# Softplus as one activation, softmax exponentials joined to decay bursts, and down products of 25 experts turned: a macaron layer on one core

## The reference

```
x = x + 0.5 * moe(layernorm(x))
x = x + mamba(layernorm(x))
x = x + 0.5 * moe(layernorm(x))          # the same weights again

moe(x):                                   # 8 experts, all of them for every token, F = 512
  router = softmax(x @ w_router);  gates = softmax(x @ w_gating / 0.1)
  h[e] = silu(x @ w_gate[e]) * (x @ w_up[e])
  cw = router * gates;  cw = cw / (sum(cw) + 1e-9)
  out = sum over e of (h[e] @ w_down[e]) * cw[:, e]

mamba(x):                                 # 256 inner channels, 16 states, conv of 4 taps
  xs, z = split(x @ W_in);  xc = silu(conv(xs) + conv_b)
  dbl = xc @ W_x;  dt = softplus(dbl[:64] @ W_dt + b_dt);  B, C = the rest of dbl
  dA = exp(dt * A), A = -exp(A_log);  dBx = dt * xc * B
  h_t = dA_t * h_(t-1) + dBx_t;  y_t = sum over states of h_t * C_t
  out = ((y + xc * D) * silu(z)) @ W_out
```

## Time and profile before

| | |
|---|---|
| median of 3 runs | 1244.83 us (1244.51 to 1245.08) |
| profiled execution, first to last instruction (span) | 1243.0 us |
| median less this span (launch and end around it) | 1.8 us |
| PE busy | 1237.4 us, 7212 products |
| DVE busy | 1143.1 us |
| ACT busy | 1004.7 us |
| POOL busy | 450.6 us |

### The profile page before, as it was taken

The page is one execution under the profiler, slowest core; times in us unless marked ns, Lnnn a source line. Parts: engine busy times, 40 slices in busy tenths (PEclk is TensorE's granted clock), DMA queues, the critical chain, the costliest instruction groups (busy, mean ns, idle before and its releaser), DMA issues.

```text
span 1243.0 us, 20366 instructions
## 1 busy us (share of the span) xinstructions
PE 1237.4 (100%) x7212; PEld 1066.6 (86%) x7212; DVE 1143.1 (92%) x1353; ACT 1004.7 (81%) x2022; POOL 450.6 (36%) x574
## 2 busy tenths in 40 slices
PE   9999999999999999999999999999999999999999
PEld 7888888888888888888888888888888888888887
DVE  5958799999998999999999999998999999998877
ACT  7678888988887989887988989898888987865554
POOL 0021144335462443543534425344453344531000
PEclk9999999999999999999999999999999999999999
DMA  8312488798877879878889787977778779881222
GB/s 232 97 30 44 86 176 176 154 184 171 168 159 155 173 150 196 168 165 165 171 175 184 162 179 149 190 163 154 153 165 175 163 155 194 169 179 35 61 52 59
DMA packets 118135, 184.59 MB, mean 148 GB/s; under 512 B 11280, under 2 KB 34448, under 8 KB 118032
## 3 DMA queue, kind: packets, MB, share of 16 engines
q0 software_dynamic: 54384, 99.11, 45.7%
q1 hardware_dynamic: 63648, 84.16, 25.3%
HBM read 81.46 MB, written 2.69 MB: 68 GB/s over the span
## 4 chain that ended last, share of the span: by engine, by line
PE 90%; ACT 3%; DVE 3%; DMA 2%; issue 2%; POOL 0%; DVEq 0%; ACTq 0%; POOLq 0%
PE PS L1070 27%; PE PS L961 18%; PE PS L964 18%; PE PS L962 18%; PE PS L1066 2%; PE PS L1062 1%; PE PS L1064 1%; PE PS L1128 1%; DMA XT<-YE 1%; DVE HB L1310 1%; PE PS L1113 1%; DMA Y<-HS 1%; PE PS L997 1%; DVE HS L1408 1%; ACT HB L1521 1%
## 5 line engine op out<-in xcount | busy, mean ns | idle before, releaser
L1070 PEld LDWEIGHTS PS<-WD,HB 128*128 128x128 f32 x3424 | 422.3, 191 | 23.7 <-issue 1.5
L1070 PE MATMUL PS<-WD,HB 128*128 128x128 f32 x3424 | 424.5, 275 | 0.0
L1310 DVE TENSOR_TENSOR HB<-PS,HB 128x1024 f32<-128x1024 f32 (+1 forms) x336 | 322.6, 961 | 77.2 <-PE PS L964 56.1
L1521 ACT ACTIVATE HB<-PS 128x512 f32<-128x512 f32 x512 | 293.6, 596 | 101.7 <-PE PS L964 99.6
L1712 POOL DMA_DIRECT2D Y<-HS x252 | 220.8, 957 | 343.8 <-DVE HS L1416 164.0
L961 PE MATMUL PS<-XH,WG 128*128 128x512 f32 x509 | 221.3, 435 | 0.0
L961 PE MATMUL PS<-XH,WU 128*128 128x512 f32 x512 | 205.3, 401 | 0.7 <-DVE HB L1310 0.5
L964 PE MATMUL PS<-XH,WU 128*128 128x512 f32 x512 | 201.2, 393 | 0.0
L964 PE MATMUL PS<-XH,WG 128*128 128x512 f32 x509 | 200.8, 395 | 0.0
L962 PE MATMUL PS<-XH,WU 128*128 128x512 f32 x512 | 200.5, 392 | 0.0
L962 PE MATMUL PS<-XH,WG 128*128 128x512 f32 x509 | 199.2, 391 | 0.0
(11 more groups left out here) (168 smaller groups left out, 1466.1 us busy)
## 6 DMA issues: line engine op xcount, KB each, us to landing
BCB<-BCD SPq DMA_DIRECT2D x128, 512.0 KB, 5.2
Y<-HS POOLq DMA_DIRECT2D x252, 256.0 KB, 6.0
XT<-YE POOLq DMA_DIRECT2D x106, 256.0 KB, 5.0
YE<-CWD SPq DMA_DIRECT2D x20, 256.0 KB, 4.5
AT<-YE POOLq DMA_DIRECT2D x14, 256.0 KB, 3.3
WD<-in_L_ffn_w_down_dram SPq DMA_DIRECT2D x8, 256.0 KB, 6.2
XT<-in_L_attn_x_dram SPq DMA_DIRECT2D x7, 256.0 KB, 6.5
out_dram<-XT SPq DMA_DIRECT2D x7, 256.0 KB, 5.7
```

Of the source, the lines that this page charges most:

```text
L1070: z = pe.matmul(part(g, j), HB[:, i % NH, j * P:(j + 1) * P], WD[:, e, c, :], start=c == 0 and j == 0, stop=c == FC - 1 and j == SUB - 1)
L1310: v.tensor_tensor(H, PS[:, NG + i % 2:NG + i % 2 + n, :], H, ALU.mult).then_inc(S["v_h"], 1)
L1521: a.activation(HB[:, i % NH, :], gate(i), ACT.Silu).then_inc(S["a_sil"], 1)
```

## The change

Three things are changed.

- Softplus is one activation. b_dt writes v + bias to DX (Identity), b_soft makes Softplus of it into XS. The sum on DVE, the accumulating DMA of tiles 1 to 3 and the list ADDED go. Decays wait for b_soft.
- The exponentials of a position's softmaxes are asked for, and the next burst of decays issues them ahead of its own, if one comes before the planner's PE clock has moved on by PATIENCE = 25; otherwise, and while no tile's decays are open, they are issued alone as before.
- TURNS has experts 1 to 7 in positions 1 and 14, 25 in all where there were 20.

```diff
-ADDED = (1, 2, 3)
-SUMMED = 10.0
+PATIENCE = 25.0
-TURNS = {0: range(2, 6), 1: range(1, 5), 14: range(3, 8), 15: range(0, 7)}
+TURNS = {0: range(2, 6), 1: range(1, 8), 14: range(1, 8), 15: range(0, 7)}
-SPLITS = {0: range(2, 6), 1: range(1, 5), 14: range(3, 8), 15: range(0, 7)}
+SPLITS = TURNS
...
         yield from calm()
-        at = step("p_exp", p, after=at, a=3.0)
+        wanted.append((p, at))
+        limit = clock["pe"] + PATIENCE
+        while p not in exp_at and decayed[0] and decayed[0] < NT * NS and clock["pe"] < limit:
+            yield False
+        if p not in exp_at:
+            wanted.clear()
+            exp_at[p] = step("p_exp", p, after=at, a=3.0)
+        at = exp_at[p]
...
-            at = step("b_dt", t, j, bk, pe=.47, a=1.1)
-            give(bk[0], "a_relu", 2 * t + j + 1, at + MARGIN)
+            at = step("b_dt", t, j, bk, pe=.47, a=.55)
+            give(bk[0], "a_pre", 2 * t + j + 1, at + MARGIN)
             yield True
         yield from calm()
-        at = step("b_soft", t, after=at, a=4.5)
+        dt_at[t] = at = step("b_soft", t, after=at, a=3.6)
         yield True
-        if t in ADDED:
-            yield from until(at)
-            at = step("b_add", t, after=at, p=.9) + SUMMED
         yield from until_v(at + LATEST)
-        at = step("b_dx", t, after=at, v=1.2 if t in ADDED else 2.4)
-        dt_at[t] = at - 1.2
+        at = step("b_dx", t, after=at, v=1.2)
...
+            if wanted and wanted[0][1] < clock["a"] + .2:
+                p, _ = wanted.pop()
+                exp_at[p] = step("p_exp", p, a=.45)
             at = step("s_da", m, after=dt_at[m // NS], a=2.56 + 1.24 * BURST)
...
-                    if t in ADDED:
-                        wt.wait_ge(S["c_dt"], 16 * (ADDED.index(t) + 1))
-                    else:
-                        wt.wait_ge(S["a_soft"], t + 1)
-                        wt.wait_ge(S["a_relu"], 2 * t + 2)
-                        v.tensor_tensor(dt, dt, dx, ALU.add).then_inc(S["v_dt"], 1)
-                        wt.wait_ge(S["v_dt"], t + 1 - sum(k < t for k in ADDED))
-                    v.tensor_tensor(dx, dt, Y[:, t % 2, :, :], ALU.mult).then_inc(S["v_dx"], 1)
+                    wt.wait_ge(S["a_soft"], t + 1)
+                    v.tensor_tensor(DX[:, t % 2, :, 0:T], XS[:, t % 2, :, 3:3 + T], Y[:, t % 2, :, :], ALU.mult
+                                    ).then_inc(S["v_dx"], 1)
...
-                    wt.wait_ge(S["v_cv"], 6 * t + 6)
-                    a.activation(DX[:, t % 2, j, 0:T], bank(b), ACT.Abs, bias=bdt_t[:, j:j + 1]).then_inc(S["a_abs"], 1)
-                    a.activation(XS[:, t % 2, j, 3:3 + T], bank(b), ACT.Relu, bias=bdt_t[:, j:j + 1]).then_inc(S["a_relu"], 1)
+                    a.activation(DX[:, t % 2, j, 0:T], bank(b), ACT.Identity, bias=bdt_t[:, j:j + 1]).then_inc(S["a_pre"], 1)
...
-                    wt.wait_ge(S["a_abs"], 2 * t + 2)
-                    a.preload_act_table_set("natural_log_exp_and_others")
-                    a.activation(dx, dx, ACT.Exp, scale=-1.0).then_inc(S["a_sexp"], 1)
-                    wt.wait_ge(S["a_sexp"], t + 1)
-                    a.activation(dx, dx, ACT.Ln, bias=1.0).then_inc(S["a_soft"], 1)
+                    wt.wait_ge(S["a_pre"], 2 * t + 2)
+                    wt.wait_ge(S["v_cv"], 6 * t + 6)
+                    a.activation(XS[:, t % 2, :, 3:3 + T], DX[:, t % 2, :, 0:T], ACT.Softplus).then_inc(S["a_soft"], 1)
...
-                elif k == "b_add":
-                    t = s[1]
-                    wt.wait_ge(S["a_soft"], t + 1)
-                    wt.wait_ge(S["a_relu"], 2 * t + 2)
-                    gp.dma_start(XS[:, t % 2, :, 3:3 + T], DX[:, t % 2, :, 0:T], accum_op=ALU.add).then_inc(S["c_dt"], 16)
```

More of the change, by code:

```diff
@@ L321, in timetable @@
     haste, inputs = set(), {0}
+    wanted, exp_at = [], {}
     stored, begun_y, put = set(), set(), {-2, -1}
@@ L706, in macaron_program @@
         S = {}
-        for n in ("c_small c_con c_wr c_acc c_y0 c_y1 c_bcd c_dt o_x init w_hi w_lo dv "
+        for n in ("c_small c_con c_wr c_acc c_y0 c_y1 c_bcd o_x init w_hi w_lo dv "
                   "m_ct m_at a_ct a_hh v_hh a_wd v_wh v_hl v_wd v_ts v_at c_ct c_cw0 c_cw1 c_cw2 m_g m_u m_dn m_tr m_lg m_win m_wx m_wt m_wo m_end v_end "
-                  "a_ye a_sil a_sum a_mean a_sq a_xn a_car a_lr a_xh a_exp a_neg a_rmh a_win a_tap a_yc a_dbl a_abs a_relu a_sexp a_soft a_yd a_da "
-                  "v_h v_mx v_norm v_cw v_ye v_mset v_rm v_halo v_cv v_bc v_db v_sc v_hc v_yz v_x2 v_dt v_dx v_y v_wr v_lt v_xl v_ve v_nm v_xn "
+                  "a_ye a_sil a_sum a_mean a_sq a_xn a_car a_lr a_xh a_exp a_neg a_rmh a_win a_tap a_yc a_dbl a_pre a_soft a_yd a_da "
+                  "v_h v_mx v_norm v_cw v_ye v_mset v_rm v_halo v_cv v_bc v_db v_sc v_hc v_yz v_x2 v_dx v_y v_wr v_lt v_xl v_ve v_nm v_xn "
                   "c_x0b m_tr0 v_mv a_sd v_x0 v_xh p_ve s_rs p_nm p_sub p_sm pl").split():
@@ L1370, in _ @@
                     t = s[1]
-                    dt, dx = XS[:, t % 2, :, 3:3 + T], DX[:, t % 2, :, 0:T]
                     wt.wait_ge(S["a_yc"], 2 * t + 2)
-                    if t in ADDED:
-                        wt.wait_ge(S["c_dt"], 16 * (ADDED.index(t) + 1))
-                    else:
-                        wt.wait_ge(S["a_soft"], t + 1)
-                        wt.wait_ge(S["a_relu"], 2 * t + 2)
-                        v.tensor_tensor(dt, dt, dx, ALU.add).then_inc(S["v_dt"], 1)
-                        wt.wait_ge(S["v_dt"], t + 1 - sum(k < t for k in ADDED))
-                    v.tensor_tensor(dx, dt, Y[:, t % 2, :, :], ALU.mult).then_inc(S["v_dx"], 1)
+                    wt.wait_ge(S["a_soft"], t + 1)
+                    v.tensor_tensor(DX[:, t % 2, :, 0:T], XS[:, t % 2, :, 3:3 + T], Y[:, t % 2, :, :], ALU.mult
+                                    ).then_inc(S["v_dx"], 1)
                 elif k == "b_dtl":
@@ L1585, in _ @@
                     wt.wait_ge(S["m_wt"], 2 * t + j + 1)
-                    wt.wait_ge(S["v_cv"], 6 * t + 6)
                     if t >= 2:
                         wt.wait_ge(S["v_db"], (t - 1) * NS)
-                    a.activation(DX[:, t % 2, j, 0:T], bank(b), ACT.Abs, bias=bdt_t[:, j:j + 1]).then_inc(S["a_abs"], 1)
-                    a.activation(XS[:, t % 2, j, 3:3 + T], bank(b), ACT.Relu, bias=bdt_t[:, j:j + 1]).then_inc(S["a_relu"], 1)
+                    a.activation(DX[:, t % 2, j, 0:T], bank(b), ACT.Identity, bias=bdt_t[:, j:j + 1]).then_inc(S["a_pre"], 1)
                 elif k == "b_soft":
                     t = s[1]
-                    dx = DX[:, t % 2, :, 0:T]
-                    wt.wait_ge(S["a_abs"], 2 * t + 2)
-                    a.preload_act_table_set("natural_log_exp_and_others")
-                    a.activation(dx, dx, ACT.Exp, scale=-1.0).then_inc(S["a_sexp"], 1)
-                    wt.wait_ge(S["a_sexp"], t + 1)
-                    a.activation(dx, dx, ACT.Ln, bias=1.0).then_inc(S["a_soft"], 1)
+                    wt.wait_ge(S["a_pre"], 2 * t + 2)
+                    wt.wait_ge(S["v_cv"], 6 * t + 6)
+                    a.activation(XS[:, t % 2, :, 3:3 + T], DX[:, t % 2, :, 0:T], ACT.Softplus).then_inc(S["a_soft"], 1)
                 elif k == "b_y":
```

## The result

The changed kernel is slower. Its median is 1254.87 us (1253.06 to 1256.95, 4 runs) against 1244.68 us of the kernel before beside it: +10.2 us, ratio 1.0078 [1.0064, 1.0093] (the bracket is the 95% interval). The forecast was 1241.0.

The account below looks back on a forecast made before the run. PE was taken as the bound, so only work taken off PE pays: -4.0 (turned products), -0.7 (Softplus bank), +0.9 (small new waits) gave -3.8, from 1244.8 to 1241.0 us, range 1238.4 to 1245.8.

Parts of the forecast that it names:

- Position 1: Three more turned experts: 10.7 us of DVE work against 8.2 us idle there, first scans 2.5 us late, PE cost 0.
- still not PE: Position 1's late scans, some 2 us if the chain doesn't get shorter, were to cost PE nothing.
- Position 14: Two more turned experts: 7.1 us of DVE work, last scans later within 29 us of room; PE cost 0, bounds 0 to +4.
- rival B: DVE becomes the bound at position 14, its rests written between tile 7's scans: +5.6, 1250 us; chance 0.11.
- The 20 us that I gave as the scans' worst delay: Position 14: delay if the remaining DVE work is served at the 18% DVE has free in turned slots.
- PE's work: Turned down products in positions 1 and 14: 20 slots at 0.20 us less each, -4.0 us, bounds -3.6 to -4.4.
- the rule of four passes: True FP32 makes four passes through the array: a quarter of 0.89 us saved per turned slot, so -4.5 us.
- Softplus: One function at 1.06 us, saving ACT 20 us over 8 tiles; only line 1590's bank touches PE, -0.7 us.
- line 1590's successor no longer releases PE: Sign expected: PE's 0.7 us wait for ACT's Relu on that bank goes, since Identity frees it earlier.
- Joined exponentials: Positions 3 to 14: ACT saves 31 us, hidden by PE; tightest at position 4, CW 2.6 us early; cost 0.
- rival D: Joined exponentials come late at position 4 or elsewhere: +3 us, then 1244.0; chance 0.21 together with a rival of partly lost savings.
- PE's waits under 3 us: Sign expected: PE's whole list of waits by engine stays under 3 us.

Follow-up runs that it names:

- e17: e15 with the 20 turned experts of the kernel before (positions 1 and 14 have 1 to 4 and 3 to 7): 1244.29 us, ratio 0.9999.
- e13: e9 with joined exponentials counted as ready 2.9 units later by the planner: 1243.15 us, ratio 0.9990.
- e8: The kernel before with experts 1 to 7 turned in position 1 and nothing else: 1253.75 us, ratio 1.0075.
- e7: The changed kernel with only experts 1 to 4 turned in position 1, and tile 2's Mamba part held until position 4 is prepared: 1247.96 us, ratio 1.0026.
- e9: The changed kernel with positions 4 and 5 exchanged, so tile 0's result is needed a position later: 1245.04 us, ratio 1.0008.
- e10: The kernel before with positions 4 and 5 exchanged and nothing else: 1255.94 us, ratio 1.0089.
- e11: e5 with experts 1 to 7 turned in position 14: 1245.89 us, ratio 1.0011.
- e5: The kernel before with only the Softplus part, and tile 2's Mamba part held until position 4 is prepared: 1244.56 us, ratio 1.0001.
- e1: The kernel before with only the Softplus part of the change: 1252.74 us, ratio 1.0065.
- e2: The kernel before with only the joining of softmax exponentials to the bursts: 1250.94 us, ratio 1.0053.
- e16: e10 with experts 1 to 6 turned in position 15 instead of 0 to 6: 1252.53 us, ratio 1.0061.
- e15: e13 with expert 7 of position 1 plain again (24 experts turned): 1242.07 us, ratio 0.9981.
- e3: The kernel before with only the turned experts (25 instead of 20): 1257.35 us, ratio 1.0103.
- e18: e15 with 22 turned experts (position 1 has 1 to 4, position 14 has 1 to 7): 1244.81 us, ratio 1.0004.
- e14: e9 with the planner's prices as traced (exponential pair 1.3 later, p_norm 4.2): 1247.46 us, ratio 1.0024.

## Why the prediction was wrong

**The step that failed** is "Position 1: ... What is left, 2.5 us, delays the first scans ... Cost for PE 0; if the chain doesn't get shorter, some 2 us of scans are late, still not PE." I set 10.7 us of new DVE work against 8.2 us of idle DVE and took the rest, 2.5 us, as the delay. The delay is 12.3 us in the profiled execution, 2.2 of them its late beginning; between e17 and e13, which begin alike, it is 13.1. Three things were wrong in the term. First, DVE's work ahead of the first scan grew by 15.8 us between these two and not by 10.7: the rests HL (8.2) and the rests of weights (2.6) are as I priced them, but I left out that DVE weighs the three turned experts (2.1), the roundings that fell to it (1.5), and the HB of the slots that pass meanwhile (3.9). Second, only 2.7 of the 9.0 us of idle time took up work. DVE's rows stand in a fixed order, and it idled for products of PE (2.04 us before 141.62 in the trace before, 1.39 us before 147.41 after). Third, I never set ACT's new roundings against ACT's own idle time. Its table load for tile 0's Softplus is at 147.19, behind the new roundings, where the load of the old form was at 139.46, and the decays that the scan reads are 12.6 us later. How much of the delay is DVE's and how much ACT's no run parts.

**The second half of that step**, "still not PE", failed too. I had checked the room of position 15 (29 us) but not that of position 4, where XH was written at 295.60, stood ready for all its uses near 299.9 and was wanted at 307.0. After the change it was written at 306.19, 10.6 us late, against 7 us of room: that is the larger part of the loss. e8 shows it alone (+9.2 us), the changed kernel is 6.9 us faster without those turned experts (e7) and 9.8 faster with the exchange (e9), though e10 shows that an exchange changes more than the room.

**Position 14** went as forecast for the scans: they end early enough, and rival B has no part in the changed kernel. But the turned slots didn't pay: e11 is 1.3 us slower than e5 where 1.6 should be saved, and PE waits 1.8 us for one HL. That is a cost of about 2.9 us, with the noise of two ratios on it, inside the 0 to +4 that I had kept and not at the 0 that I took. The 20 us that I gave as the scans' worst delay was also low by its own working: 4.6 us of work at 18% is 25 us, still under the 29.

**PE's work**: forecast -4.0, found -4.3 (3.4 to 4.5 by other ways to take the usual spacing); new turned slots in position 14 start at 1129.36 and 1131.44, 2.08 us apart, as in the earlier trace rows. Lines 1070 and 1062 to 1066 have the counts forecast. By the rule of four passes, as the prediction cites it from the Trainium skill ("FP8 and Floating Point Precision", TensorE Precision Notes), it would have been -4.5, by the rows -4.0; what was found can't tell them apart.

**Softplus**: 1061 ns against the 1.06 taken, with its load of 1283 ns. Its effect on the time, -0.7 forecast, isn't seen (e5: 0.0, interval -1.0 to +1.4). The wait for that bank is still in the list of the changed kernel (line 1126 for ACT's line 1588, the Identity, 0.7 us in two), so "line 1590's successor no longer releases PE" was wrong. The gap ahead of tile 2's scans did shrink, from 16.3 to 5.7 us, but tile 1's scans end late, so tile 2's begin at 403.4 and not 401.6.

**Joined exponentials**: I priced the tightest one from the times before (CW at 324.3, wanted at 326.90). That held only while position 4 kept its own time. With tile 0 late CW was begun at 335.63, and rival D's mechanism did act, as a consequence: 1.62 us of DVE, 1.92 and 1.88 of PE. Loads fell from 180 to 156, as forecast.

**The order as a cost.** No rival had the case that less work makes the kernel slower, and e1 is it: 8 us for two norms exchanged. It isn't the changed kernel's loss, yet it was the loss of either smaller change (e1, e2). "PE's waits under 3 us" failed; "I would be wrong most plainly if PE's idle time grew while its count of products fell as computed" is what came.

**What stays open.** Of the 15.1 us of waits and slow spacing, most of the 5.9 in position 4 have their rows (waits of 1.92, 1.88 and 0.80 us), and the edits against the delay of tile 0 take 7 to 10 us away from the whole. The 2.2 us of position 0 belong to one execution. The 1.7 us each of positions 2 and 7 weren't looked into. Almost every new order was slower than the one before, whatever its edit (e1, e2, e8, e10, e16), so the order before may be one that happened to suit; no run tests that in general. Nor is it known why e15's order avoids the wait of position 9, or what costs e10 all of the rest.

## What to carry to other kernels

When instructions are written out in a fixed order, don't subtract an engine's idle time from new work. Here 15.8 us more work ahead of the first scan used up 2.7 of 9.0 us of idle time, and the rest came out as delay. So list the hand-overs, the places where one tile's chain must meet the main line, read the room of each from the trace, and follow a delay to the nearest one, not to the one that looks fullest. Where a planner writes the order, test each edit also with the order pinned at those places, since taking work away can exchange two chains; and give room first (here a position's exchange), then spend it.

## What the runs showed of the hardware

- A short wait of PE can be paid twice. Three waits with 2.9 us in all (e8), one of 5.0 us (e1) and one of 4.7 (e10) were followed by a granted clock of 0.57, 0.61 and 0.66 over the 8 us from where PE went on (in e8 after the first of the three). Single waits of 2.53 us (e3, at 1164.80), 2.42 (e18) and 2.30 (e17) were followed by 0.79. But the length of the wait doesn't settle it: after a wait of 2.44 us in e14 (160.49) the clock stayed at 1.00, and so it did after those of 1.92 and 1.88 us in the changed kernel's position 4, while one of 1.75 us in e16 (1145.62) was followed by 0.79.
- Softplus exists as one function of ACT at the price of any other of its shape: 1061 ns for 128x1024 against 1062 for the Ln. It brings its own load. The Trainium skill ("ScalarE: Activation LUTs", What ACT_TABLE_LOAD costs) gives a switch as a load of 1283 ns and about 1.38 us of drain; here the trace differs. The row ahead of the load for tile 0's Softplus ends at 147.17, the load begins at 147.19 and the function at 148.48, so the switch there costs 1.31 us in all. The median over all loads of this trace is the same 1.31 us.
- A chain of small operations on POOL is dear, and its price varies: p_norm, seven operations on at most 128x48, takes 2.05 us in position 0 and 2.05 to 5.15 us over the positions of the traces before and after. Its first two operations took 1.38 and 1.30 us in position 4 and 0.25 and 0.29 in position 0. Why they vary wasn't tested.
